# Four-head attention of a two-layer kernel: only high and low query parts are turned, and ScalarE writes the high parts a second time out of the same PSUM bank

## What is computed

```
xn = layernorm(x)
s  = attention(xn)                    # layer 0: causal, one head; layer 1: chunked, 16 heads
g  = silu(ffn(xn))                    # layer 0: mixture of 8 experts; layer 1: see below
x  = x + s * g
```

```
Q  = (nx @ Wq.T) as 4 heads of 32      # nx = rmsnorm(xn, g1)
Kc = nx @ Wkc.T ; Vc = nx @ Wvc.T      # one key and one value of 32 for each row
scores = Q . Kc / sqrt(32) ; attn = softmax(scores) ; out = attn @ Vc @ Wo.T
```

## Time and profile before

| | |
|---|---|
| median of 3 runs | 661.65 us (659.08 to 662.32) |
| the profiled execution | 661.58 us |
| its span (first to last instruction) | 659.8 us |
| granted TensorE clock, mean | 0.97 |
| TensorE matmuls busy | 596.2 us, 90% |
| VectorE busy | 466.8 us, 71% |
| GpSimd busy | 370.3 us, 56% |
| ScalarE busy | 353.7 us, 54% |

### The profile page before, as it was taken

One profiled execution on the slowest core, in us unless ns is written; L12 is line 12 of the kernel. 1 busy time (PEld: TensorE's weight loads), 2 busy tenths in 40 slices (PEclk: granted clock), 3 DMA queues, 4 the chain that ended last, 5 costly groups with the idle time before them and its releaser, 6 DMA issues.

```text
span 659.8 us, 12615 instructions
## 1 busy us (share of the span) xinstructions
PE 596.2 (90%) x4528; PEld 403.4 (61%) x4529; DVE 466.8 (71%) x1097; ACT 353.7 (54%) x710; POOL 370.3 (56%) x421
## 2 busy tenths in 40 slices
PE   4886789973998899996999999999999999999996
PEld 2564689953766456664655555555555553688885
DVE  5755344431897878889877777787777784788986
ACT  2643355532486454552677676677667667433221
POOL 6607400056254943371788888898889879514211
PEclk9989799996999999997899999999999999999999
DMA  9701112111000000000000000000000000000101
GB/s 304 320 1 45 36 38 75 48 48 32 2 0 1 2 2 2 2 2 2 0 1 1 1 0 1 1 1 1 0 2 1 1 1 1 1 1 1 33 0 33
DMA packets 16617, 17.34 MB, mean 26 GB/s; under 512 B 1712, under 2 KB 15024, under 8 KB 16176
## 3 DMA queue, kind: packets, MB, share of 16 engines
q1 hardware_dynamic: 15536, 14.49, 6.4%
q0 software_dynamic: 1024, 2.10, 1.1%
HBM read 11.34 MB, written 5.24 MB: 25 GB/s over the span
## 4 chain that ended last, share of the span: by engine, by line
PE 73%; DVE 11%; POOL 4%; ACT 4%; another core or an unknown queue 4%; issue 3%; DMA 1%; SPq 0%; DVEq 0%; ACTq 0%; POOLq 0%
PE ps L2085 12%; PE ps L2075 10%; PE ps L2065 8%; PE ps L2213 5%; PE ps L1795 4%; PE ps L1888 3%; DVE region L1118 3%; PE ps L1878 3%; PE ps L1778 3%; PE ps L2203 3%; PE ps L2205 2%; PE ps L2204 2%; PE ps L1976 2%; PE ps L1992 1%
## 5 line engine op out<-in xcount | busy, mean ns | idle before, releaser
L1118 DVE TENSOR_REDUCE region<-ps 128x1 f32<-128x512 f32 x256 | 160.2, 685 | 51.7 <-PE ps L2065 51.4
L1568 ACT ACTIVATE region<-ps 128x512 f32<-128x512 f32 x256 | 137.9, 598 | 52.2 <-PE ps L2075 51.8
L777 POOL TENSOR_TENSOR region<-region 128x512 f32<-128x512 f32 x80 | 106.8, 1339 | 22.7 <-ACT region L1568 19.7
L2075 PE MATMUL ps<-qmr,kr 98*128 98x512 f32 x256 | 111.4, 439 | 1.7 <-ACT region L1568 0.8
L2065 PE MATMUL ps<-kr,qmr 96*128 96x512 f32 x256 | 101.9, 410 | 0.6 <-DVE region L1118 0.3
L2085 PE MATMUL ps<-region 128*32 128x512 f32 x512 | 91.8, 599 | 0.0
L2092 PE MATMUL ps<-region,ones 128*32 128x512 f32 x192 | 91.6, 598 | 0.2 <-DVE region L1134 0.2
L782 POOL TENSOR_TENSOR region<-region 128x512 f32<-128x512 f32 x64 | 82.0, 1282 | 11.9 <-ACT region L1568 7.9
L2075 PEld LDWEIGHTS ps<-qmr,kr 98*128 98x128 f32 x256 | 49.0, 192 | 53.5 <-issue 23.7
L1795 PE MATMUL ps<-region 128*128 128x128 f32 x272 | 41.2, 301 | 23.2 <-ACT region L1418 15.1
L2065 PEld LDWEIGHTS ps<-kr,qmr 96*128 96x128 f32 x256 | 49.7, 195 | 11.3 <-DVE region L1118 4.3
(11 more groups left out here) (287 smaller groups left out, 1189.5 us busy)
## 6 DMA issues: line engine op xcount, KB each, us to landing
region<-in_w SPq DMA_DIRECT2D x2, 2048.0 KB, 12.6
slots_in<-zeros SPq DMA_DIRECT2D x1, 1536.0 KB, 8.9
region<-slots_in SPq DMA_DIRECT2D x6, 256.0 KB, 2.8
slots_out<-og SPq DMA_DIRECT2D x6, 256.0 KB, 2.4
e<-in_e SPq DMA_DIRECT2D x1, 1152.0 KB, 15.5
x<-in_x SPq DMA_DIRECT2D x4, 256.0 KB, 3.6
out<-y SPq DMA_DIRECT2D x3, 256.0 KB, 2.3
e<-in_e SPq DMA_DIRECT2D x1, 576.0 KB, 16.7
```

Of the source, the lines that this page charges most:

```text
L777: ins = pool.tensor_tensor(o, held(tiles[0]), held(tiles[1]), ALU.add)
L1118: dve.tensor_reduce(mxp[:, u // HM, u % HM:u % HM + 1], bank(b), AX.X, ALU.max).then_inc(mx_read, 1)
L1568: act.activation(pm[:, t // 2, t % 2 * HM * P:(t % 2 + 1) * HM * P], bank(SCORE_BANKS[n % 3]), ACT.Exp, scale=SCM).then_inc(p_whole, 1)
L2075: pe.matmul(bank(SCORE_BANKS[n % 3]), kr[0:M_ROWS, t * P:(t + 1) * P], rows_of(i)[0:M_ROWS, :], start=True, stop=True).then_inc(st_filled, 1)
```

## The change

`qtile2` loses the second copy of the high parts: a head is now high, low and the two maximum columns (66 in place of 98). TensorE turns 64 rows in place of 96. ScalarE copies these 64 rows, and with a second instruction the first 32 rows of the same bank (the high parts) into rows 64 to 95 of `rows_of(i)`. So the row order of the queries is now high, low, high, and the keys are laid out as high, high, low to match. The semaphore `tile_ready` is gone; who waited for it waits for `q_high_ready`.

```diff
+Q_ROWS = 2 * DM
+Q_COLS = Q_ROWS + 2
...
-        qtile2 = sb("qtile2", [P, 2, HM, M_ROWS], F32R)
+        qtile2 = sb("qtile2", [P, 2, HM, Q_COLS], F32R)
...
-                pool.tensor_copy(ka[:, r, 2 * DM:3 * DM], ka[:, r, 0:DM]).then_inc(ka_ready, 1)
-                pool.tensor_tensor(ka[:, r, DM:2 * DM].bitcast(F32R), kv, ka[:, r, 0:DM], ALU.subtract).then_inc(ka_ready, 1)
+                pool.tensor_copy(ka[:, r, DM:2 * DM], ka[:, r, 0:DM]).then_inc(ka_ready, 1)
+                pool.tensor_tensor(ka[:, r, 2 * DM:3 * DM].bitcast(F32R), kv, ka[:, r, 0:DM], ALU.subtract).then_inc(ka_ready, 1)
...
-                pool.tensor_tensor(qtile2[:, parity, :, 2 * DM:3 * DM], q, qtile2[:, parity, :, 0:DM].bitcast(F32),
+                pool.tensor_tensor(qtile2[:, parity, :, DM:2 * DM], q, qtile2[:, parity, :, 0:DM].bitcast(F32),
                                    ALU.subtract).then_inc(q_low_ready, 1)
...
-                dve.wait_ge(tile_ready, i + 1)
+                dve.wait_ge(q_high_ready, i + 1)
...
                 act.wait_ge(q_turned, i - 1)
-                act.activation(rows_of(i)[0:R_ROWS, :], bank(7)[0:R_ROWS, :], ACT.Copy).then_inc(qm_ready, 1)
+                act.activation(rows_of(i)[0:Q_ROWS, :], bank(7)[0:Q_ROWS, :], ACT.Copy)
+                act.activation(rows_of(i)[Q_ROWS:R_ROWS, :], bank(7)[0:DM, :], ACT.Copy).then_inc(qm_ready, 1)
...
                 act.activation(qtile2[:, parity, :, 0:DM], q, ACT.Copy).then_inc(q_high_ready, 1)
-                act.activation(qtile2[:, parity, :, DM:2 * DM], q, ACT.Copy).then_inc(tile_ready, 1)
...
                 act.wait_ge(f_filled, fill_of["query", i] + 1)
-                act.activation(rows_of(i)[0:R_ROWS, :], bank(1)[0:R_ROWS, :], ACT.Copy).then_inc(f_drained, 1)
+                act.activation(rows_of(i)[0:Q_ROWS, :], bank(1)[0:Q_ROWS, :], ACT.Copy)
+                act.activation(rows_of(i)[Q_ROWS:R_ROWS, :], bank(1)[0:DM, :], ACT.Copy).then_inc(f_drained, 1)
...
-                pe.wait_ge(tile_ready, i + 1)
+                pe.wait_ge(q_high_ready, i + 1)
                 pe.wait_ge(q_low_ready, i + 1)
                 seven(qm_ready, i + 1)
                 for h in range(HM):
-                    ins = pe.matmul(bank(7)[0:R_ROWS, P * h:P * (h + 1)], qtile2[:, parity, h, 0:R_ROWS], ident_r[:, :], start=True, stop=True)
+                    ins = pe.matmul(bank(7)[0:Q_ROWS, P * h:P * (h + 1)], qtile2[:, parity, h, 0:Q_ROWS], ident_r[:, :], start=True, stop=True)
```

More of the change, by code:

```diff
@@ L390, in bass_recurrent_two_layers @@
         mx_filled = sem("mx_filled"); mx_read = sem("mx_read"); m_turned = sem("m_turned")
-        tile_ready = sem("tile_ready"); q_turned = sem("q_turned"); qm_ready = sem("qm_ready")
+        q_turned = sem("q_turned"); qm_ready = sem("qm_ready")
         sum_step = sem("sum_step"); sum_ready = sem("sum_ready"); last_sum_ready = sem("last_sum_ready"); oT_ready = sem("oT_ready"); o_turned = sem("o_turned")
@@ L803, in low_maximum @@
             def low_maximum(i, parity):
-                high, low = (qtile2[:, parity, :, R_ROWS + n] for n in range(2))
+                high, low = (qtile2[:, parity, :, Q_ROWS + n] for n in range(2))
                 pool.wait_ge(m_step, i * MSTEPS + 2)
@@ L1127, in high_maximum @@
                 dve.wait_ge(m_step, i * MSTEPS + 1)
-                dve.tensor_copy(qtile2[:, parity, :, R_ROWS], negm[:, :]).then_inc(m_step, 1)
+                dve.tensor_copy(qtile2[:, parity, :, Q_ROWS], negm[:, :]).then_inc(m_step, 1)
             def last_sum(i):
@@ L1155, in query_tile @@
                 dve.wait_ge(q_high_ready, i + 1)
-                dve.tensor_tensor(qtile2[:, parity, :, 2 * DM:3 * DM], q, qtile2[:, parity, :, 0:DM].bitcast(F32),
+                dve.tensor_tensor(qtile2[:, parity, :, DM:2 * DM], q, qtile2[:, parity, :, 0:DM].bitcast(F32),
                                   ALU.subtract).then_inc(q_low_ready, 1)
@@ L1166, in _ @@
             dve.wait_ge(m_step, 2)
-            dve.tensor_tensor(qtile2[:, 0, :, R_ROWS + 1], negm[:, :], qtile2[:, 0, :, R_ROWS].bitcast(F32), ALU.subtract).then_inc(m_step, 1)
+            dve.tensor_tensor(qtile2[:, 0, :, Q_ROWS + 1], negm[:, :], qtile2[:, 0, :, Q_ROWS].bitcast(F32), ALU.subtract).then_inc(m_step, 1)
             chunk_out(NT - 1)
@@ L2050, in turn_maxima @@
                 for h in range(HM):
-                    ins = pe.matmul(bank(7)[0:M_ROWS - R_ROWS, P * h:P * (h + 1)], qtile2[:, parity, h, R_ROWS:M_ROWS], ident_r[:, :], start=True, stop=True)
+                    ins = pe.matmul(bank(7)[0:M_ROWS - R_ROWS, P * h:P * (h + 1)], qtile2[:, parity, h, Q_ROWS:Q_COLS], ident_r[:, :], start=True, stop=True)
                 ins.then_inc(m_turned, 1)
@@ L2103, in first_queries @@
                 o = fill("query", i)
-                pe.wait_ge(tile_ready, i + 1)
+                pe.wait_ge(q_high_ready, i + 1)
                 pe.wait_ge(q_low_ready, i + 1)
                 for h in range(HM):
-                    ins = pe.matmul(o[0:R_ROWS, P * h:P * (h + 1)], qtile2[:, i, h, 0:R_ROWS], ident_r[:, :], start=True, stop=True)
+                    ins = pe.matmul(o[0:Q_ROWS, P * h:P * (h + 1)], qtile2[:, i, h, 0:Q_ROWS], ident_r[:, :], start=True, stop=True)
                 ins.then_inc(f_filled, 1)
```

## The result

| | before | after |
|---|---|---|
| median of 6 runs | 661.49 us (659.08 to 662.54) | 667.24 us (666.73 to 669.69) |
| ratio, 95% interval | | 1.0092 (1.0064 to 1.0119) |
| the profiled execution | 661.58 us | 666.98 us |
| its span | 659.8 us | 665.2 us |

The change makes the kernel 0.9% slower, 5.75 us between the medians. The forecast was 663.2 us, the range ended at 666.4, and the slower rival stood at 665.5. The sign was right, the size was not: 5.75 us in place of 1.65.

A forecast was written before the change was run, and what follows sets the result against it. In the four-head stage the chain of waits never leaves TensorE, so its time was taken to bound the kernel. From 661.58 us, 3.7 - 0.95 - 1.1 = +1.65 gave 663.2 us, range 659.6 to 666.4.

The forecast's parts named there:

- the slower rival: ScalarE between exponents of slots 5 and 6: second drain costs its full 0.60 us, total 665.5 us; chance 0.20.
- The second drain: ScalarE between exponents of slots 5 and 6, 14 tiles: the added drain delays slot 6's exponent by 0.49 us.
- the bound of 0.60: Upper bound on the second drain's cost in us, assuming no overlap with its neighbours on ScalarE.
- Slot 11: TensorE waits there for GpSimd's low part: 0.35 us in nine tiles, 0.07 in tile 8, nothing in four.
- the prediction's own sum: TensorE's wait at slot 11: drain 0.49 plus least distance 0.09 minus existing distance 0.23, giving 0.35 us.
- The 0.05 added for what comes behind a wait: TensorE at slot 11: a wait costs more than its length, as matmuls behind it run slower; 0.05 us each.
- the term: Total TensorE loss at slot 11 from the second drain: 9 x 0.40 + 0.12 = +3.7 us.
- The removed copy: Tile start: dropping ScalarE's 0.20 us copy frees slots 2 and 3, 0.19 us in five tiles, -0.95 us.
- My bound below, "0": The least gain allowed for removing the copy at the tile's start; the other bound was 5 x 0.20.
- 64 rows turned: TensorE turning queries with 64 instead of 96 rows: 0.07 us gained per tile, 14 tiles plus chunk stage's two, -1.1 us.
- Chunk stage: ScalarE gets 0.6 us more work; L1545 starts about 0.1 us later, covered by 1 us: costs nothing, bounds 0 and 0.4.
- the one without a wait: TensorE at slot 11 runs loads and scores behind the maxima instead of waiting; only gains stay, 659.5 us; chance 0.10.

The follow-up runs named there:

- e5: The changed kernel with two more unread drains of bank 7 ahead of its own two, seven kinds over tiles 2 to 15; ran once, 682.42 us.
- e4: The kernel before with a second drain of 32 rows from bank 7 into a spare tile, nothing else changed; 667.07 us, ratio 1.0081.
- e1: The changed kernel with ScalarE's 0.2 us copy at the tile's start put back, into an unread spare tensor; 664.70 us, ratio 1.0042.
- e6: The kernel before with its second query copy moved from the tile's start to behind the exponent of slot 3; 663.00 us, ratio 1.0024.
- e8: The changed kernel with VectorE's `last_sum` moved from slot 1 to slot 0; 665.78 us, ratio 1.0086.
- e9: The changed kernel with TensorE turning the maxima at slot 12, ScalarE's drain unmoved, and `last_sum` at slot 0; 661.64 us, ratio 1.0010.
- e10: The changed kernel with VectorE making the second copy from bank 7 at slot 8, and `last_sum` at slot 0; 662.41 us, ratio 1.0002.
- e2: The changed kernel with `TURN_SLOT` 12 instead of 11, moving TensorE's turning of the maxima and ScalarE's drain; 674.12 us, ratio 1.0190.

## Why the prediction was wrong

**The second drain: the failed step is "A copy of 32 rows over 512 columns has the same 512 columns to go through, so I take 0.49 us for it".** It costs 0.72, more than the bound of 0.60. The reason given against the slower rival, "no pair of ScalarE's neighbours here shows such a gap", was not true of the trace of before. The drain of the maxima, two rows written at row 96, stands there with 0.61 us to the exponent behind it, and starts 0.63 behind the exponent ahead of it. ScalarE's timeline of the kernel before, slot 11 of tile 5:

```profile
400.87 1.08 ACT L1568 ACTIVATE region<-ps 128x512 f32<-128x512 f32 x2
401.98 0.58 ACT L1556 ACTIVATE qmr<-ps 2x512 fp32r<-2x512 f32 x1
402.59 0.60 ACT L1568 ACTIVATE region<-ps 128x512 f32<-128x512 f32 x1
```

I took the pitch from the drain that was to be replaced, which begins at row 0 like the exponents around it, and not from the one that, like the new drain, lands further down. The Trainium skill (ScalarE: Activation LUTs, What ACT_TABLE_LOAD costs) says that back-to-back ACTIVATEs overlap by about 93 ns. The exponents here come near that (0.60 us long, 0.49 apart, an overlap of 0.11); the pairs in e5 that change their first row don't (0.59 long, 0.58 to 0.61 apart).

**Slot 11: right mechanism, wrong size.** With 0.72 the prediction's own sum gives 0.72 + 0.09 - 0.23 = 0.58 of wait and 0.63 of delay; measured are 0.48 to 0.58 of delay in nine tiles, where 0.40 was forecast. The 0.05 added for what comes behind a wait was not seen, and from GpSimd's end to L2054 it is 0.05 (353.84 to 353.89), not 0.09. Tiles 5, 9, 12 and 13, which were to have no wait, have 0.13 to 0.23, and tile 8, which was to have 0.12, has none. The latter has lost its time already: at slot 8 it waits for GpSimd's piece 1 (L784), which was in no step of the prediction. e4, with the second drain alone, shows it too; how the drain comes to delay that piece was not followed. The timeline of the kernel after:

```profile
448.51 0.14 PEld L2095 LDWEIGHTS ps<-region,ones 128*32 128x32 f32 x2 [0.61 <-POOL region L784]
```

So the term was +3.7 and is +5.5 at slot 11 with tile 0, and +0.4 to +0.9 at slot 8.

**The removed copy: the failed step is "Removing the wait gives 0.09 + 0.10 = 0.19 us", in five tiles.** The first half, at slot 2, came in all five. The second came in tiles 8 and 12; in 5, 7 and 11 it became a wait of some 0.8 us. In all +1.96 us (slots 2 and 3) in place of -0.95. I had asked who waits for ScalarE behind the copy and found TensorE; I did not ask who else does. GpSimd's first addition does, and the trace of before shows it 0.07 us behind VectorE's. e1, e6 and e8 turn the order at will, and VectorE's addition goes between 0.7 and 1.7 us with it. The Trainium skill (SBUF — State Buffer, Who interferes with whom) says that VectorE with two SBUF inputs contends with a GpSimd instruction that reads SBUF, that the shared port pair is an exclusive lock, and that the order of issue decides who blocks. The trace agrees: VectorE's addition, when it is second, ends 0.55 us behind the end of GpSimd's in tile 5 of the kernel after, which is most of its own 0.68. My bound below, "0", excluded a loss, and no reason stood for that.

**64 rows turned: right.** -0.07 us in each tile, -0.98 over 13 of them. The groups of weight loads, 316 to 536 us, after, beside the earlier trace rows:

```profile
L2045 PEld LDWEIGHTS ps<-ident_r,qtile 128*64 128x64 f32 x56 | 5.3, 136 | 3.5 <-issue 1.9
```

The chain of waits of the kernel after, 335 to 365 us, has 0.24 for the four pairs, where it was 0.32:

```profile
348.78 0.24 PE ps L2045 x4
```

**Chunk stage: covered, as forecast, with the size off in the same way.** L1547 starts 1.21 us behind the first drain (279.54 to 280.75), its counterpart before the change 0.90 behind the one drain (281.29 to 282.19): 0.3 us later, where 0.1 was forecast. TensorE's product that reads it (L2011, at 282.42) still starts 0.64 us behind its end, with no wait for ScalarE before it.

**The rivals.** The slower one had the place and nearly the time (665.5), in part by luck: its sum left out the overlap lost on the second side of the drain, took 0.15 us from GpSimd to the matmul where 0.05 was measured, and set the gain at slot 3 against it. Its reason, that a second read of the same bank cannot start before the first ends, doesn't hold: in e5 two drains of bank 7 from the same row start 0.49 us apart. Of the one without a wait nothing was seen: no weight load behind L2054 was pulled ahead of the load that waited (at slot 11 of tile 2 the next one, L2078's, starts at 354.07, behind all of L2054's four, the first at 353.89). A slip of the range: that rival's own time, 659.5, lies just below the 659.6 that was said to take it in.

**The sum.** 7.06 us in tiles 1 to 14 and 5.75 between medians don't have to agree: the profile of before had TensorE at half its clock from about 37 to 41 us, that of after did not. Their windows, 36 to 41 us, before and then after: busy time of PE, PEld, DVE, ACT, POOL, then the granted clock (0.66, and 1.00).

```profile
36.00:41.00 5.00, 5.00 (x24) 3.97 (x25) 3.04 (x8) 1.19 (x2) 0.00 (x0) 0.66 0.00 0
```
```profile
36.00:41.00 5.00, 5.00 (x39) 4.45 (x39) 3.38 (x9) 2.48 (x4) 0.00 (x0) 1.00 0.00 0
```

The same instruction of ScalarE is at 33.0 us before and 32.4 after, and behind the stretch at 41.5 and 39.3: 1.5 us were lost there. With this and smaller differences the first score of the stage was 1.9 us later before the change (310.1 us) than after (308.2), and the spans differ by 5.4 us. Nearly all of this lies in parts that the change doesn't touch; what it costs in its own stage is the 7 us.

## What to carry to other kernels

When an operation is removed ahead of several consumers, look at each of them and not only at the one that waits for it in the trace: what comes 0.2 us earlier may take a shared resource from a neighbour that was ahead by 0.07. When an instruction is added, take its price from the instruction that is most like it in where it reads and writes, and count what it does to the pitch on both of its sides. And a slot table of one engine, differenced between two profiles, shows in one look what the sum over a stage hides.

## What the runs showed of the hardware

- Two ScalarE instructions over 512 columns that begin at the same row start 0.48 to 0.50 us apart, with 32, 64, 96 or 128 rows; where the first row read or written differs from one to the next, 0.58 to 0.61.
- A VectorE addition of 128x512 out of SBUF took 0.68 us when it started 0.07 us before GpSimd's, and 1.74 when it started 0.10 behind it. GpSimd's, 1.28 us long when it is first, took 1.75 when it was the second by 0.07.
- Some profiles have a stretch of about 3 us near the end of the stage in which TensorE's granted clock was 0.50, the 1.2 GHz level: e1, e4, e9 and e10 in tile 15, where one slot (8 or 14) is 1.6 us longer than before the change, and e2 in tile 14. They are no part of what these kernels do differently. In e1 TensorE's matmuls were busy without a gap in it; in the 2 us before it fell they were busy 1.69 us. The windows of e1, 558 to 561 us:

```profile
558.00:561.00 3.00, 3.00 (x17) 0.45 (x9) 0.00 (x0) 1.14 (x3) 2.53 (x3) 0.50 0.00 0
```

  The kernels before and after ran these matmuls at 1.00. When such a stretch comes was not settled; each is worth some 1.6 us, as much as the whole forecast (+1.65), and is a reason to read sums slot by slot.
